# A gated cross-attention and expert layer on one core: other layouts and queues for the first loads, the first norm in pairs, the gates spread by DMA

## What is computed

```
x = x + tanh(g_xattn[0]) * xattn(layernorm(x), ctx, Wq, Wk, Wv, Wo, bo)
x = x + tanh(g_ffn[0])   * ffn(layernorm(x), gate_w, w1, b1, w2, b2)

xattn: q = x @ Wq ; k = ctx @ Wk * 64**-0.5 ; v = ctx @ Wv      (16 heads of 64)
       softmax(q k^T) v, joined, @ Wo + bo
ffn:   router = softmax(mean over tokens(h) @ gate_w) ; top 2 of 8 experts per sequence
       sum over the two of weight * (gelu(h @ w1[e] + b1[e]) @ w2[e] + b2[e])
```

## Time and profile before

| | |
|---|---|
| median of 3 runs | 321.79 us (321.60 to 321.92) |
| profiled execution, its own time | 322.05 us |
| its span | 320.0 us |
| TensorE (PE) busy | 315.3 us, 99% |
| weight load (PEld) busy | 273.0 us, 85% |
| VectorE (DVE) busy | 234.7 us, 73% |
| ScalarE (ACT) busy | 164.1 us, 51% |
| GpSimd (POOL) busy | 78.9 us, 25% |
| granted TensorE clock | 1.0 |
| moved by DMA | 17.35 MB, mean 54 GB/s |

### The profile page before, as it was taken

How to read it: one execution, slowest core, us unless ns; L and a number is a source line. 1 busy time by engine, 2 the same in 40 slices (tenths; PEclk the granted TensorE clock), 3 DMA queues, 4 the chain that set the end, 5 groups by cost and what they waited for, 6 DMA issues and landing times.

```text
span 320.0 us, 5745 instructions
## 1 busy us (share of the span) xinstructions
PE 315.3 (99%) x1881; PEld 273.0 (85%) x1881; DVE 234.7 (73%) x563; ACT 164.1 (51%) x577; POOL 78.9 (25%) x158
## 2 busy tenths in 40 slices
PE   8999999999999999999999999999999999999996
PEld 8978998889999999888788888888887899888896
DVE  1889999988889999999998475466767554442643
ACT  2648566686765768766466254444543442321320
POOL 1325554784465536425600000000000000000000
PEclk9999999999999999999999999999999999999999
DMA  7991000000000027500007250000020000000011
GB/s 276 382 161 6 0 3 0 0 3 3 0 0 3 0 80 237 213 1 0 2 7 256 70 195 1 0 0 0 19 101 14 2 0 2 0 0 0 2 66 66
DMA packets 20765, 17.35 MB, mean 54 GB/s; under 512 B 11068, under 2 KB 16900, under 8 KB 20612
## 3 DMA queue, kind: packets, MB, share of 16 engines
q1 hardware_dynamic: 20464, 16.51, 17.2%
q10 hardware_dynamic: 276, 0.52, 0.5%
HBM read 14.93 MB, written 2.10 MB: 53 GB/s over the span
## 4 chain that ended last, share of the span: by engine, by line
PE 96%; DVE 1%; DMA 1%; POOL 1%; issue 0%; ACT 0%; DVEq 0%
PE ps L1105 28%; PE ps L1107 27%; PE ps L1106 27%; PE ps L1190 4%; PE ps L1125 2%; PE ps L1279 1%; PE ps L1221 1%; DMA ctx_sb<-in_ctx_dram 1%; PE ps L1163 1%; PE ps L1377 1%; PE ps L1147 1%; POOL sx L473 1%; DVE a_lo L759 0%; PE ps L1101 0%; DVE sm L824 0%
## 5 line engine op out<-in xcount | busy, mean ns | idle before, releaser
L674 ACT ACTIVATE gel<-ps,b1sel 128x512 f32<-128x512 f32 x64 | 43.9, 690 | 95.5 <-PE ps L1107 95.4
L1064 DVE CAST h_hi<-gel 128x512 fp32r<-128x512 f32 x64 | 28.4, 443 | 58.8 <-ACT gel L674 58.5
L587 ACT ACTIVATE sx<-ps,mx 128x64 f32<-128x64 f32 x128 | 38.3, 327 | 26.7 <-DVE mx L855 26.7
L1105 PE MATMUL ps<-yT_hi,w_hi 128*128 128x512 f32 (+1 forms) x128 | 50.5, 395 | 0.0
L1106 PE MATMUL ps<-yT_lo,w_hi 128*128 128x512 f32 (+1 forms) x128 | 50.0, 390 | 0.0
L1107 PE MATMUL ps<-yT_hi,w_lo 128*128 128x512 f32 (+1 forms) x128 | 49.9, 390 | 0.0
L1066 DVE TENSOR_TENSOR h_lo<-gel,h_hi 128x512 fp32r<-128x512 f32 x64 | 44.9, 702 | 2.2
L473 POOL TENSOR_TENSOR sx<-sx,rs 128x512 f32<-128x512 f32 x32 | 33.2, 1058 | 47.6 <-DVE rs L829 47.4
L1105 PE MATMUL ps<-h_hi,w_hi 128*128 128x512 f32 x96 | 38.4, 400 | 0.0
L1107 PE MATMUL ps<-h_hi,w_lo 128*128 128x512 f32 x96 | 37.5, 390 | 0.0
L1106 PE MATMUL ps<-h_lo,w_hi 128*128 128x512 f32 x96 | 37.4, 390 | 0.0
(11 more groups left out here) (145 smaller groups left out, 670.3 us busy)
## 6 DMA issues: line engine op xcount, KB each, us to landing
stage_w<-in_L_ffn_w_dram SPq DMA_DIRECT2D x7, 1024.0 KB, 7.3
out_dram<-xt SPq DMA_DIRECT2D x6, 256.0 KB, 2.6
wqT<-in_L_xattn_Wq_dram SPq DMA_DIRECT2D x2, 512.0 KB, 7.0
wv_sb<-in_L_xattn_Wv_dram SPq DMA_DIRECT2D x2, 512.0 KB, 8.6
wo_sb<-in_L_xattn_Wo_dram SPq DMA_DIRECT2D x1, 1024.0 KB, 13.3
xt<-in_x_dram SPq DMA_DIRECT2D x1, 1024.0 KB, 10.4
stage_w<-in_L_ffn_w_dram SPq DMA_DIRECT2D x2, 512.0 KB, 4.4
wk_sb<-in_L_xattn_Wk_dram ACTq DMA_DIRECT2D x1, 512.0 KB, 4.7
```

Source lines behind the costliest of these rows:

```text
L587: last = nc.scalar.activation(sx[:, par, c0:c0 + M], ps[:, 2 * par + 1, c0 - BANK:c0 - BANK + M], ACT.Exp, bias=mx[:, par, h:h + 1], accum ...
L674: nc.scalar.activation(gel[:, f % 4, :], ps[:, h_bank, :], ACT.Gelu, bias=b1sel[:, b, slot, f:f + 1]).then_inc(gelu_done, 1)
L1064: nc.vector.tensor_copy(h_hi[:, f % 4, :], gel[:, f % 4, :]).then_inc(hhi_ready, 1)
L1105: mm(acc, hi_w, hi_x, start=start, stop=False)
```

## The change

- The context is laid out transposed by the host and loaded as `ctxT`; its transposes and their copy go, with the ctxT group. The banks of the groups are dealt anew. TensorE does eight warm-ups and then the keys.
- Wk is laid out and loaded in four quarters, 1 and 2 by SP, 0 and 3 by ACT. A kT group waits for a quarter at its start and for the next in its middle. x's tiles 0 and 1 are now loaded by ACT between its two quarters.
- The gates are loaded into all 128 partitions (source step 0), the tanh is taken on all of them, by ACT between kT 0 and kT 1; its one-row matmul and DVE's copy go.
- `X_PARTS` has four parts: 2, 2, 4 and 8 tiles. Part 0's whole norm comes after its own two statistics. The guess for part 1 comes behind A's low parts and the second `x_low`, and its Newton rounds stand on POOL ahead of tile 2's normalisation. Of the four statistics of tiles 4 to 7, two move to step 0.

```diff
-            sp.dma_start(ctx_sb[:, :], ctx_tokens.rearrange("b m d -> (b m) d")).then_inc(ld_ctx, 16)
-            load_x(0, 0, 0, 2)
-            sp.dma_start(wk_sb[:, :, HD // 2:HD], Wk[1].rearrange("k p n -> p k n")).then_inc(ld_wk[1], 16)
+            sp.dma_start(ctxT[:, :, :, :], ctx_tokens).then_inc(ld_ctx, 16)
+            for quarter in (1, 2):
+                sp.dma_start(wk_sb[:, quarter, :, :], Wk[quarter]).then_inc(ld_wk[quarter], 16)
             load_x(1, 0, 2, TB // 2)
...
-            act.dma_start(wk_sb[:, :, 0:HD // 2], Wk[0].rearrange("k p n -> p k n")).then_inc(ld_wk[0], 16)
-            act.dma_start(gg[:, 0:1], g_xattn.rearrange("(o n) -> o n", o=1)).then_inc(ld_g, 16)
-            act.dma_start(gg[:, 1:2], g_ffn.rearrange("(o n) -> o n", o=1)).then_inc(ld_g, 16)
+            act.dma_start(wk_sb[:, 0, :, :], Wk[0]).then_inc(ld_wk[0], 16)
+            act.dma_start(xt[:, 0:2, :], x_block(0, 0, 2)).then_inc(ld_x[0], 16)
+            act.dma_start(wk_sb[:, 3, :, :], Wk[3]).then_inc(ld_wk[3], 16)
+            for i, g in enumerate((g_xattn, g_ffn)):
+                act.dma_start(gg[:, i:i + 1], g.rearrange("(o n) -> o n", o=1).broadcast_to([P, 1])).then_inc(ld_g, 16)
...
-            act.wait_ge(ld_g, 32)
-            nc.scalar.activation(tg_row[:, :], gg[:, :], ACT.Tanh).then_inc(tanh_done, 1)
...
             group("kT", 0)
+            act.wait_ge(ld_g, 32)
+            nc.scalar.activation(tg[:, :], gg[:, :], ACT.Tanh).then_inc(tg_ready, 1)
             group("kT", 1)
...
-        GRP_BANK = dict(zip(groups, [0, 1, 2, 3, 4, 5, 6, 0, 1, 3, 4, 2, 6, 4, 5, 0, 6] + [0, 1] * len(LATE)))
+        GRP_BANK = dict(zip(groups, [5, 6, 0, 2, 3, 4, 5, 6, 1, 2, 3, 6, 4, 5, 0, 6] + [0, 1] * len(LATE)))
...
-        X_PARTS = [(0, TB // 2), (TB // 2, TB), (TB, NT)]
-
-        X_BY_DVE = X_PARTS[1][0]
+        X_PARTS = [(0, 2), (2, TB // 2), (TB // 2, TB), (TB, NT)]
+
+        X_BY_DVE = X_PARTS[2][0]
...
+                if s == -1:
+                    newton(*X_PARTS[1], rstd1, ve_x, 2)
                 if s == 1:
-                    newton(*X_PARTS[1], rstd1, ve_x, 2)
+                    newton(*X_PARTS[2], rstd1, ve_x, 3)
...
-            group("ctxT", 0)
             x_stats(0, range(0, 2))
+            x_norm(0)
             x_stats(1, range(2, TB // 2))
-            x_norm(0)
-            dve.wait_ge(tg_spread, 1)
-            nc.vector.tensor_copy(tg[:, :], ps[:, 7, 0:2]).then_inc(tg_ready, 1)
...
             x_low(1)
-            x_stats(2, range(TB // 2, TB))
+            x_norm(1)
+            x_stats(2, range(TB // 2, TB // 2 + 2))
...
                     group("vT", 1)
+                    x_stats(2, range(TB // 2 + 2, TB))
                     out_bias(0)
-                    x_norm(1)
+                    x_norm(2)
...
-                if kind == "ctxT":
-                    pe.wait_ge(ident_ready, 1)
-                    pe.wait_ge(ld_ctx, 16)
+                pe.wait_ge(ld_ctx, 16)
+                if kind == "vT":
+                    pe.wait_ge(ld_wv[i], 16)
+                for m in range(4):
+                    quarter, c0 = 2 * i + m // 2, (4 * i + m) * P
+                    if kind == "kT" and m % 2 == 0:
+                        pe.wait_ge(ld_wk[quarter], 16)
...
-            warm_up(6)
-            group("ctxT", 0)
-            warm_up(3)
+            warm_up(8)
             group("kT", 0)
             group("kT", 1)
-            pe.wait_ge(rows_ready, 1)
-            pe.wait_ge(tanh_done, 1)
-            mm(ps[:, 7, 0:2], ones_row[:, :], tg_row[:, :], start=True, stop=True).then_inc(tg_spread, 1)
```

More of the change, by code:

```diff
@@ L17, in gated_cross_attention_moe_kernel @@
     P = 128
-    B, M, D = ctx_tokens.shape
-    S = out.shape[0] // B
+    _, _, B, M = ctx_tokens.shape
+    S, D = out.shape[0] // B, out.shape[1]
     HD = 2 * Wv.shape[-1]
@@ L78, in gated_cross_attention_moe_kernel @@
     nu = place("nu", [P, TB])
-    gg = place("gg", [1, 2])
-    tg_row = place("tg_row", [1, 2])
+    gg = place("gg", [P, 2])
     tg = place("tg", [P, 2])
@@ L113, in gated_cross_attention_moe_kernel @@
     first = [cursor[0]]
-    wk_sb = place("wk_sb", [P, KD, HD], at=first)
+    wk_sb = place("wk_sb", [P, 4, KD, HD // 4], at=first)
     wv_sb = place("wv_sb", [P, KD, HD], at=first)
@@ L119, in gated_cross_attention_moe_kernel @@
     vT_sb = place("vT_sb", [P, NP, B, M], at=first)
-    ctx_sb = place("ctx_sb", [P, D], at=first)
-    ctxT = place("ctxT", [P, KD, P], at=first)
+    ctxT = place("ctxT", [P, KD, B, M], at=first)
     first2 = [cursor[0]]
@@ L175, in gated_cross_attention_moe_kernel @@
         ld_wq = [sem(f"ld_wq_{i}") for i in range(2)]
-        ld_wk = [sem(f"ld_wk_{i}") for i in range(2)]
+        ld_wk = [sem(f"ld_wk_{i}") for i in range(4)]
         ld_x = [sem(f"ld_x_{i}") for i in range(4)]
@@ L184, in gated_cross_attention_moe_kernel @@
         bias_done = sem("bias_done")
-        tanh_done, tg_spread, tg_ready = sem("tanh_done"), sem("tg_spread"), sem("tg_ready")
+        tg_ready = sem("tg_ready")
         grp_done, grp_act, grp_dve = sem("grp_done"), sem("grp_act"), sem("grp_dve")
@@ L298, in gated_cross_attention_moe_kernel @@
         late_groups = [(kind, i + odd) for kind, i in LATE.values() for odd in range(2)]
-        setup_groups = [("ctxT", 0), ("kT", 0), ("kT", 1)]
-        groups = setup_groups + A0 + V0 + late_groups
+        groups = [("kT", 0), ("kT", 1)] + A0 + V0 + late_groups
         number = {g: n for n, g in enumerate(groups)}
-        GRP_BANK = dict(zip(groups, [0, 1, 2, 3, 4, 5, 6, 0, 1, 3, 4, 2, 6, 4, 5, 0, 6] + [0, 1] * len(LATE)))
+        GRP_BANK = dict(zip(groups, [5, 6, 0, 2, 3, 4, 5, 6, 1, 2, 3, 6, 4, 5, 0, 6] + [0, 1] * len(LATE)))
         assert all(s % 2 == 1 for s in LATE)
@@ L749, in group @@
                 bank = ps[:, GRP_BANK[(kind, i)], :]
-                if kind == "ctxT":
-                    dve.wait_ge(grp_done, n + 1)
-                    nc.vector.tensor_copy(ctxT[:, :, :], bank[:, 0:D].rearrange("p (k i) -> p k i", k=KD)).then_inc(grp_dve, 1)
                 if kind == "vT":
@@ L879, in step @@
                 if s == 4:
-                    x_norm(2)
+                    x_norm(3)
                 if s == 14:
@@ L1112, in group @@
                     wait_group_read(pe, *GRP_BEFORE[(kind, i)])
-                if kind == "ctxT":
-                    pe.wait_ge(ident_ready, 1)
-                    pe.wait_ge(ld_ctx, 16)
-                    for k in range(KD):
-                        last = nc.tensor.transpose(bank[:, k * P:(k + 1) * P], ctx_sb[:, k * P:(k + 1) * P], ident[:, :])
-                if kind in ("kT", "vT"):
-                    w_sb = wk_sb if kind == "kT" else wv_sb
-                    pe.wait_ge(ld_wk[i] if kind == "kT" else ld_wv[i], 16)
-                    wait_group_read(pe, "ctxT", 0)
-                    for m in range(4):
-                        for k in range(KD):
-                            c0 = (4 * i + m) * P
-                            last = mm(bank[:, m * P:(m + 1) * P], w_sb[:, k, c0:c0 + P], ctxT[:, k, :],
-                                      start=(k == 0), stop=(k == KD - 1))
+                pe.wait_ge(ld_ctx, 16)
[5 more added lines that the diff above has]
+                        pe.wait_ge(ld_wk[quarter], 16)
+                    for k in range(KD):
+                        w = wk_sb[:, quarter, k, m % 2 * P:(m % 2 + 1) * P] if kind == "kT" else wv_sb[:, k, c0:c0 + P]
+                        last = mm(bank[:, m * P:(m + 1) * P], w, ctxT[:, k, :, :].rearrange("p b j -> p (b j)"),
+                                  start=(k == 0), stop=(k == KD - 1))
                 last.then_inc(grp_done, 1)
@@ L1215, in step @@
                     if t == 0:
-                        pe.wait_ge(tg_ready, 1)
+                        pe.wait_ge(ident_ready, 1)
                     wait_pos(pe, ylo_ready, len([1 for at in (Y_WITH_X, Y_AFTER) for n in at if n < s]))
@@ L1445, in _laid_out @@
         a = a.T.reshape(2, -1, 128, a.shape[0]).transpose(0, 2, 1, 3)
-    if name in ("L0_xattn_Wk", "L0_xattn_Wv"):
+    if name == "ctx_1024":
+        a = a.transpose(2, 0, 1).reshape(-1, 128, *a.shape[:2]).transpose(1, 0, 2, 3)
+    if name == "L0_xattn_Wk":
+        a = a.reshape(a.shape[0] // 128, 128, 4, -1).transpose(2, 1, 0, 3)
+    if name == "L0_xattn_Wv":
         a = a.reshape(a.shape[0] // 128, 128, 2, -1).transpose(2, 0, 1, 3)
```

2 lines of the change are left out of this document (1 added, 1 removed).

## The result

| | before | after |
|---|---|---|
| median of 6 runs each, on one chip | 321.82 us | 324.97 us (324.60 to 326.22) |
| ratio | | 1.0107, 95% interval 1.0094 to 1.012 |
| profiled execution, its own time | 322.05 us | 324.85 us |
| its span | 320.0 us | 322.8 us |

The change makes the kernel 3.15 us slower; I forecast 321.2, in a range of 320.6 to 322.1. The span says the same (+2.8), and it was lost before 31 us. The scores of tile 2 start on TensorE at 31.20, where they started at 28.23.

A forecast was written before the change was run, and what follows sets the result against it. TensorE, busy 63.89 of 64 us after the start, was taken to pass on any change before about 28 us. The sum -1.03 (start) + 0.45 (give-back) = -0.58 gave 321.2 us, range 320.6 to 322.1.

The forecast's parts named there:

- TensorE's keys: Keys' projection on TensorE: starts at 4.85 and ends at 9.43, bounds 9.2 to 9.7, against 10.23 before.
- the change of pace: TensorE's clock during the keys: instructions go from 0.213 to 0.112 us each near 6.9, as before.
- The 2.2 MB: Loads on both queues ahead of Wq's first half: at 404 GB/s it lands at 9.4, the A product's earliest start.
- The pair's norm: DVE's norm of x's first two tiles: 2.83 us, from 8.96 to 11.79 in old times, as long as for four.
- The stall at tile 2's transposes: TensorE wants tile 2 at 23.80, POOL has it normalised at 24.55 (old times): a stall of 0.75.
- The slow clock between Wk's quarters: Rival: TensorE's waits for weights keep the keys at 0.213 us per instruction, 323.4 us; chance 0.07.
- a term put at nothing: Gates' DMAs on ACT's queue: 256 pieces of 4 bytes cost 0.1 us, nothing against 0.8 MB ahead; landing near 8.
- gates late: Rival: gates landing after about 9.8 hold up ACT's tanh, kT 1 and every a_hi, 322.5 us; chance 0.06.
- the start hardly moves: Rival: late x, quarter one or Wq leave 0.3 to 0.5 of gain, which is given back, 321.8 us; chance 0.19.
- my signs of being wrong: First A matmul after 10, keys' matmuls of 0.4 us beyond 8, ACT waiting past 9.8, no wait for xn.
- the give-back of the norm: Later guess and statistics on DVE and late tile 2 from POOL return 0.45 of the gain, range 0.3 to 0.6.
- the 1.03 of the A product: Start of the A product: about 9.5 in place of 10.54, gaining 1.03 if DVE is ready for a_lo.

The follow-up runs named there:

- 322.46: The changed kernel with only the gates' part undone (one element each, early tanh, one-row spread matmul): 322.46 us, ratio 1.0019 to the kernel before.
- 321.17: The changed kernel with gates and norm both as before, leaving the transposed context and Wk's quarters: 321.17 us, ratio 0.9977 to the kernel before.
- the split done well: Changed kernel with gates as before, second pair's guess ahead of A's low parts, POOL held until it ends: 320.87 us, ratio 0.9972 to the kernel before.

## Why the prediction was wrong

**Right, or near.** TensorE's keys: I had an end at 9.43 with bounds of 9.2 to 9.7; it was 8.95, below them. I had kept the change of pace at the old 6.9, and it came sooner (eight instructions from 5 to 6, twelve from 6 to 7; before, six from 6 to 7). It brought nothing, because Wq wasn't there. The 2.2 MB that I put ahead of Wq's first half are 1.7 MB and that half itself; the 9.4 stays the same by it. The pair's norm: 2.83 forecast, 6.47 to 9.28 measured. x's first pair landed even before my bounds of 6.2 to 6.9, its statistics start at 5.69. The stall at tile 2's transposes: 0.75 forecast, ended by POOL's xn, 0.57 measured (0.60 with the gates as before). The two statistics behind the vT copy take up DVE's 0.35 idle, as costed. The slow clock between Wk's quarters didn't come.

**Wrong, and most of the miss: the gates.** The step that failed is a term put at nothing. It said that the small bias loads move 2,500 pieces per us, "so 256 are 0.1 us: nothing against the 0.8 MB ahead of them", and "I put their landing near 8". Both gates had landed at 12.2. The row I had taken for the price is of pieces with addresses of their own; these 256 read two addresses. Nor was it a matter of the tanh, which was my rival "gates late" (322.5): the kernel without its wait is no faster. It was the other loads that came late, Wq's first half above all, which "at the same 404 GB/s" I had at 9.4; it landed at 11.0, and TensorE stood for 2.21. The gates' part cost 2.5 us in all, 2.1 of it by the first a_lo. The other 0.4, DVE's idle before `sm`, stands nowhere in the prediction, and its cause is open. The rival "the start hardly moves" did name Wq slipping "by half a microsecond behind the 256 pieces"; it slipped by 1.6. I counted the bytes ahead of Wq and the pieces of the gates apart from each other, and gave the effect of the one on the rate of the other no price from a row. Two of my signs of being wrong came (a first A matmul later than 10, ACT waiting past 9.8), the keys' slow matmuls beyond 8 did not.

**Wrong: the give-back of the norm.** The step shifted every old duration: eight instructions are 1.1 us. But it had itself worked out that POOL would normalise tiles 2 and 3 up to 25.8, over the guess for tiles 4 to 7, and didn't put the two timelines beside each other. The guess took 2.21 for 1.05, and `vw` behind it came so late that TensorE waited for it too (0.89; 0.48 with the gates as before), a wait that my sum doesn't have. By the kernels at 322.46 and 321.17 the split costs 1.3 where I had 0.45.

**Mis-sized: the start.** I took the 1.03 of the A product as the gain "if DVE is ready", with a_lo due at 11.3. With the gates and the norm as before DVE was ready at 11.62, and 0.65 came through. With the split done well a_lo comes at 11.02, and 0.99 comes through. That the kernel at 321.17 lies on my forecast of 321.2 is luck: its sum has neither my start nor my give-back.

In this order the parts are -0.65 for the start, +1.3 for the norm's split and +2.5 for the gates. That they give +3.15 is no test, since each is the difference of two kernels in a row; in another order they have other sizes: the gates alone cost the kernel before only 1.2.

## What to carry to other kernels

Cost a DMA by what it does to the loads that run beside it, and not by its own bytes and pieces alone; a broadcast of one element from DRAM into all partitions goes behind the loads that something waits for, or is made on the chip from one element. When a step is moved on GpSimd, lay its new interval over VectorE's: a chain of small dependent instructions there can double in length (1.05 to 2.2 us here) without waiting for any semaphore. And when the start of a pipeline becomes faster on one engine, look at once for who is ready second, since the gain is theirs to give: here DVE, then POOL.
